# Moving the mixing matrices of a two-layer conditional residual kernel from GpSimd to VectorE

## The chip, the core and the metric

The kernel runs on one core of a Trainium2 chip. The metric is the device time of one launch in microseconds (us), here the median of three runs. The engines of the core work side by side and meet only at semaphores: TensorE (PE; its weight loads are PEld), VectorE (DVE), ScalarE (ACT), GpSimd (POOL) and SyncE (SP), which here only issues DMAs.

## What is computed

There are 64 samples of 128 channels by 2048 positions, in float32. Both layers add their result to their input:

```
# layer 0: grouped convolution, 4 groups of 32 channels, 9 taps, plus a context column
x = x + conv1d(x, weight, groups=4, padding=4) + (c @ c_weight.T)[:, :, None] + bias[None, :, None]
# layer 1: per sample a mix of K = 8 matrices of 128 x 128
h   = gelu(c @ W0 + b0);  h = gelu(h @ W1 + b1);  att = softmax(h @ W2 + b2)       # [64, 8]
agg_w = einsum('bk,koi->boi', att, weight[..., 0]);  agg_b = att @ bias_k
x = x + einsum('boi,bih->boh', agg_w, x) + agg_b[:, :, None]
```

So each sample needs its own matrix of 128 x 128: the sum of eight fixed matrices, each times one attention weight, plus the identity for the residual. This is the **mixing matrix**. The attention weights and the bias column of all samples stand in `table`, 9 columns per sample.

## The kernel before, in words

**Precision.** TensorE works on a rounded type, so each operand is split in two: a rounded value ("hi") and its rest ("lo" = value minus hi). A product is hi*hi + hi*lo + lo*hi. For x, `x_hi` and `x_lo`; for the first layer's output y, `y_hi` and `y_lo`; the mixing matrix is stored as `mix_parts[., 0]` (hi) and `[., 1]` (lo).

**Stages of one sample s.** SP loads x(s) into `x_in`. ACT turns it into four phases, `x_ph` (`split_phases`, L508). DVE rounds it, `x_hi` (`round_x`, L595), and takes the rest, `x_lo` (`rest_x`, L601). PE convolves (`conv_step`, L429): 36 steps for each of four output phases g, the four running side by side in four row groups and each two steps behind the one before. The last 12 of the 36 steps read `x_lo`. ACT rounds the result out of PSUM, `y_hi` (`round_y`, L521), and DVE takes its rest, `y_lo` (`rest_y`, L612), four instructions each. The PSUM bank of phase g is free for the convolution of s+1 when `y_lo(s, g)` is made. Two samples later PE multiplies y by the mixing matrix (`mix_step`, L460, 12 steps per phase), and ACT adds the bias column from `par` and writes `z_out` (`take_z`, L534), which SP stores.

**The order.** Each engine runs the same software pipeline: a `slot` per sample, slots 0 to 7 written out, 8 to 59 in a hardware loop, the rest written out. An engine works through its slots strictly in order, so an instruction that waits holds up all behind it. Per slot s the order is: PE convolves s, then mixes s-2; ACT takes z(s-3), splits x(s+2), rounds y(s); DVE rounds x(s+1), takes the rest of x(s+1), then the four rests of y(s); SP loads the mixing matrix of s-1, stores z(s-3), loads x(s+4), stores the matrix of s. `x_in`, `x_ph`, `x_hi`, `x_lo` have two buffers each, so ACT may split x(s+2) only when `x_lo(s)` is made (the wait `x_lo_made` in `split_phases`).

**The mixing matrix** is made by GpSimd alone (`mix_matrix`, L731 to L763), for every sample: a copy of the sample's 9 columns to `par` (L734), two products of 128x512 (L739), a tree of three sums (L744 twice, L747), the identity added twice (L751, L754), and the rest (L757). It goes through DRAM (`mix_dram`) to be replicated into four row groups (`mix_rep`, four DMAs, L290), and TensorE needs it two slots after the sample's convolution. A `par` buffer is reused after four samples (the wait on `z_read`).

**The start.** During the convolution of sample 0 the small network runs between its steps. DVE fills the attention columns of `table` (L664) and, after the four rests of y(0), finishes the bias column (`finish_table`, L676 to L680), upon which GpSimd copies it to `par[0]` (L763).

Of the kernel before, what the change touches and what calls it, by code (L numbers as in the profile page):

```python
# [5 lines left out]
F32 = mybir.dt.float32  # L6
# [48 lines left out]
def cond_resid_kernel(nc, x, cond, bias, conv_w, ctx_w, w0, b0, w1, b1, w2, b2, mix_w, mix_b, out):  # L55
# [15 lines left out]
    with ExitStack() as stack:  # L71
        def sb(name, shape, dt=F32):
            return stack.enter_context(nc.sbuf_tensor(name, shape, dt))

        def sem(name):
            return stack.enter_context(nc.semaphore(name))
# [125 lines left out]
        par_made = sem("par_made")  # L202
        par_first = sem("par_first")
        prod_made = sem("prod_made")
        mix_sum = sem("mix_sum")
        mix_hi_made = sem("mix_hi_made")
        mix_made = sem("mix_made")
# [42 lines left out]
        def _(sp):  # L250
            def ahead(*values):

                for v in values:
                    if not isinstance(v, int):
                        sp.compute_val(v)
                return values
# [11 lines left out]
            def store_mix(s):  # L268

                if not exists(s):  # L270
                    return
                b = buf(s)
                made, taken = ahead(done(s), DMA * G * uses(s))
                sp.wait_ge(mix_made, made)

                at_least(sp, mix_loaded[b], taken)
                sp.dma_start(mix_dram[b][:, :, :], mix_parts[b][:, :, :].bitcast(F32)).then_inc(mix_stored[b], DMA)
# [310 lines left out]
        def _(dve):  # L588
# [42 lines left out]
            def rest_half(h):  # L631
# [39 lines left out]
                                    ALU.add).then_inc(table_made, 1)  # L671
            rest_x((0, 1))

            def finish_table():
                dve.wait_ge(table_made, 2)
                nc.vector.tensor_tensor(aggb_prod, aggb_prod, table[:, :, 0:NK], ALU.mult).then_inc(table_made, 1)  # L676
                dve.wait_ge(table_made, 3)
                nc.vector.tensor_reduce(agg_b[:, :], aggb_prod, AX.X, ALU.add).then_inc(table_made, 1)
                dve.wait_ge(table_made, 4)
                nc.vector.tensor_tensor(table[:, :, NK:NK + 1].rearrange("p s a -> p (s a)"), agg_b[:, :],  # L680
                                        ctx_c[:, :], ALU.add).then_inc(table_made, 1)
# [26 lines left out]
        def _(pool):  # L708
# [15 lines left out]
            def mix_matrix(s):  # L724

                if not exists(s):
                    return

                at_least(pool, z_read, done(s, 2, lag=-U))
                if is_sample(s, 0):  # L730
# [16 lines left out]
                nc.gpsimd.tensor_tensor(mix_sum_f[:, :], mix_prod[:, 0, :], mix_prod[:, 1, :],  # L747
                                        ALU.add).then_inc(mix_sum, 1)
                pool.wait_ge(mix_sum, done(s, 3))

                nc.gpsimd.tensor_tensor(mix_f[:, :], mix_sum_f[:, :], ident[:, :], ALU.add)  # L751

                at_least(pool, mix_stored[buf(s)], DMA * uses(s))
# [3 lines left out]
                nc.gpsimd.tensor_tensor(mix_parts[buf(s)][:, 1, :], mix_f[:, :],  # L757
                                        mix_parts[buf(s)][:, 0, :].bitcast(F32),
                                        ALU.subtract).then_inc(mix_made, 1)
                pool.wait_ge(mix_made, done(s))  # L760
                if is_sample(s, 0):
                    pool.wait_ge(table_made, 5)
                    nc.gpsimd.tensor_copy(par[0][:, NK:PC], table[:, 0, NK:PC]).then_inc(par_made, 1)  # L763
# [27 lines left out]
```

## Time and profile before

| | |
|---|---|
| median of 3 runs | 729.33 us (728.32 to 730.14) |
| profiled execution, own time | 728.89 us |
| its span | 726.9 us |
| PE busy | 716.2 us, 99% |
| PEld busy | 701.7 us, 97% |
| DVE busy | 462.2 us, 64% |
| ACT busy | 601.3 us, 83% |
| POOL busy | 546.9 us, 75% |
| mean granted TensorE clock | 0.998 |

The span goes from the first to the last instruction; some 2 us of the execution lie around it. Busy time is the time in which an engine had an instruction running, waits inside an instruction included. TensorE's matmuls overlap, so a busy PE need not be at its peak; idle weight loads show a stall sooner.

### The profile page before, as it was taken

The numbers are of one execution on the slowest core, as the hardware profiler recorded it, in microseconds if no ns is written. First come the engines' busy times: TensorE is split into PE (matmuls) and PEld (weight loads), VectorE is DVE, ScalarE is ACT, GpSimd is POOL, SyncE is SP. The second block draws the span as 40 slices with busy tenths as digits, with TensorE's granted clock in tenths as the row PEclk, the third lists the DMA queues.
The fourth block names the chain that finished last, engine by engine and source line by source line (L and its number), as shares of the span: only waits on it lengthen the run. The fifth ranks groups of instructions, "written<-read, shape, count | busy, mean of one in ns | idle before, by whom it ended". The sixth has DMA issues, their size and how long they took to land.

```text
span 726.9 us, 29222 instructions
## 1 busy us (share of the span) xinstructions
PE 716.2 (99%) x12417; PEld 701.7 (97%) x12417; DVE 462.2 (64%) x411; ACT 601.3 (83%) x458; POOL 546.9 (75%) x592
## 2 busy tenths in 40 slices
PE   8999999999999999999999999999999999999996
PEld 6799999999999999999999999999999999999996
DVE  4897676576776675575575575575575575575543
ACT  5988888878888888888988888888888988888843
POOL 2799999999999999967767767767767767767750
PEclk9999999999999999999999999999999999999999
DMA  6345858768777877877787778777777767767546
GB/s 208 140 152 200 274 202 281 244 213 298 251 250 261 274 253 248 285 244 246 268 280 260 251 272 294 244 238 275 245 242 275 245 238 275 245 243 271 191 151 243
DMA packets 66551, 177.56 MB, mean 244 GB/s; under 512 B 7437, under 2 KB 50008, under 8 KB 50264
## 3 DMA queue, kind: packets, MB, share of 16 engines
q1 hardware_dynamic: 66002, 176.93, 71.5%
q8 instruction: 25, 0.41, 0.2%
q10 hardware_dynamic: 518, 0.17, 0.1%
q14 instruction: 6, 0.05, 0.0%
HBM read 101.57 MB, written 75.50 MB: 244 GB/s over the span
## 4 chain that ended last, share of the span: by engine, by line
PE 81%; POOL 11%; DMA 5%; SPq 1%; issue 1%; DVE 0%; ACT 0%; DVEq 0%; POOLq 0%; ACTq 0%
PE ps L429 60%; PE ps L460 21%; POOL mix_prod L744 4%; POOL mix_prod L739 4%; DMA mix_dram<-mix_parts 3%; POOL mix_sum_f L747 1%; DMA x_in<-in_x_dram 1%; SPq L290 1%; POOL mix_f L751 1%; DMA mix_rep<-mix_dram 1%; POOL mix_parts L757 1%; POOL mix_parts L754 0%; POOL par L734 0%; POOL par L763 0%; ACT x_hi L512 0%
## 5 line engine op out<-in xcount | busy, mean ns | idle before, releaser
L429 PE MATMUL ps<-x_hi,cw_hi 32*128 32x512 f32 x3072 | 406.0, 387 | 0.8 <-ACT x_hi L512 0.5
L429 PE MATMUL ps<-x_hi,cw_lo 32*128 32x512 f32 x3072 | 405.0, 386 | 0.0
L508 ACT ACTIVATE x_ph<-x_in 128x2560 f32<-128x2560 f32 x63 | 318.7, 5060 | 2.7 <-DMA x_in<-in_x_dram 2.2
L612 DVE TENSOR_TENSOR y_lo<-ps,y_hi 128x512 fp32r<-128x512 f32 x256 | 159.1, 683 | 241.1 <-ACT y_hi L521 241.1
L429 PE MATMUL ps<-x_lo,cw_hi 32*128 32x512 f32 x3072 | 275.6, 385 | 0.0
L429 PEld LDWEIGHTS ps<-x_lo,cw_hi 32*128 32x128 f32 x3072 | 240.0, 183 | 2.3 <-issue 0.8
L429 PEld LDWEIGHTS ps<-x_hi,cw_hi 32*128 32x128 f32 x3072 | 219.5, 184 | 3.8 <-issue 1.6
L429 PEld LDWEIGHTS ps<-x_hi,cw_lo 32*128 32x128 f32 x3072 | 219.1, 184 | 1.6 <-issue 0.2
L460 PE MATMUL ps<-y_hi,mix_rep 32*128 32x512 f32 x2048 | 215.1, 384 | 2.1 <-DMA mix_rep<-mix_dram 2.1
L534 ACT ACTIVATE z_out<-ps,par 128x1024 f32<-128x1024 f32 x124 | 146.5, 1242 | 74.5 <-PE ps L460 74.5
L601 DVE TENSOR_TENSOR x_lo<-x_ph,x_hi 128x2560 fp32r<-128x2560 f32 x63 | 190.0, 3016 | 2.1
L460 PEld LDWEIGHTS ps<-y_hi,mix_rep 32*128 32x128 f32 x2048 | 182.3, 183 | 4.3 <-issue 1.8
L744 POOL TENSOR_TENSOR mix_prod<-mix_prod 128x512 f32<-128x512 f32 (+1 forms) x128 | 165.3, 1291 | 10.0
L521 ACT ACTIVATE y_hi<-ps 128x512 fp32r<-128x512 f32 x256 | 132.9, 603 | 32.1 <-PE ps L429 32.0
L460 PE MATMUL ps<-y_lo,mix_rep 32*128 32x512 f32 x1024 | 158.1, 384 | 0.0
L739 POOL TENSOR_TENSOR mix_prod<-mixw_t,par 128x512 f32<-128x512 f32 x128 | 147.2, 1171 | 5.2
L734 POOL COPY par<-table 128x9 f32 (+1 forms) x63 | 68.9, 1094 | 108.0 <-ACT z_out L534 102.2
L460 PEld LDWEIGHTS ps<-y_lo,mix_rep 32*128 32x128 f32 x1024 | 125.2, 183 | 0.6
L595 DVE CAST x_hi<-x_ph 128x2560 fp32r<-128x2560 f32 x63 | 100.9, 1601 | 0.3 <-ACT x_ph L508 0.3
L747 POOL TENSOR_TENSOR mix_sum_f<-mix_prod 128x128 f32<-128x128 f32 x64 | 45.4, 710 | 5.0
L751 POOL TENSOR_TENSOR mix_f<-mix_sum_f,ident 128x128 f32<-128x128 f32 x64 | 40.8, 637 | 5.0
L754 POOL TENSOR_TENSOR mix_parts<-mix_sum_f,ident 128x128 fp32r<-128x128 f32 x64 | 39.9, 623 | 0.0
(79 smaller groups left out, 94.9 us busy)
## 6 DMA issues: line engine op xcount, KB each, us to landing
x_in<-in_x_dram SPq DMA_DIRECT2D x64, 1024.0 KB, 7.0
out_dram<-z_out SPq DMA_DIRECT2D x63, 1024.0 KB, 5.0
mix_rep<-mix_dram SPq DMA_DIRECT2D x256, 128.0 KB, 2.7
mix_dram<-mix_parts SPq DMA_DIRECT2D x64, 128.0 KB, 5.7
out_dram<-x_in SPq DMA_DIRECT2D x2, 512.0 KB, 4.0
z_out<-in_L_cond_weight_dram SPq DMA_DIRECT2D x1, 512.0 KB, 4.0
cw_nat<-in_L_cond_weight_dram SPq DMA_DIRECT2D x1, 144.0 KB, 2.2
w_sb<-in_L_cond_W_dram ACTq DMA_DIRECT2D x2, 64.0 KB, 5.0
```

The lines of the kernel that those rows point to most:

```text
L429: mm = pe.matmul(y_at(s)[:, g, :], w[rows, m, :], x_at(xx[buf(s)], rows, m), start=i == 0, stop=i == CONV - 1)
L460: mm = pe.matmul(z_at(s)[:, r, :], rep_at(s)[rows, g, h, :], yy[s[1]][rows, g, :], start=i == 0, stop=i == MIX - 1)
L508: nc.scalar.activation(x_ph[buf(s)][:, :, :, :], by_lane(x_in[buf(s)]), ACT.Copy).then_inc(x_split_ph, 1)
L521: nc.scalar.activation(y_hi[s[1]][:, g, :], y_at(s)[:, g, :], ACT.Copy).then_inc(y_hi_made, 1)
L534: nc.scalar.activation(out_lanes(z_out[buf(s)], pair), z_lanes(z_at(s), pair), ACT.Identity, bias=par[s[1]][:, NK:NK + 1]).then_inc(z_read, 1)
L595: nc.vector.tensor_copy(x_hi[buf(s)][:, :, :, :], x_ph[buf(s)][:, :, :, :]).then_inc(x_hi_made, 1)
L601: nc.vector.tensor_tensor(x_lo[buf(s)][:, :, :, :], x_ph[buf(s)][:, :, :, :], x_hi[buf(s)][:, :, :, :].bitcast(F32), ALU.subtract).then_in ...
L612: nc.vector.tensor_tensor(y_lo[s[1]][:, g, :], y_at(s)[:, g, :], y_hi[s[1]][:, g, :].bitcast(F32), ALU.subtract).then_inc(y_lo_made, 1)
L734: nc.gpsimd.tensor_copy(par[s[1]][:, :], table[:, number(s), :]).then_inc(par_made, 1)
L739: nc.gpsimd.tensor_tensor(mix_prod[:, ks, :], mixw_t[:, ks, :], par[s[1]][:, ks].unsqueeze(2).broadcast_to([P, NK // 2, P]), ALU.mult).the ...
L744: nc.gpsimd.tensor_tensor(mix_prod[:, 0:half, :], mix_prod[:, 0:half, :], mix_prod[:, half:2 * half, :], ALU.add).then_inc(mix_sum, 1)
L747: nc.gpsimd.tensor_tensor(mix_sum_f[:, :], mix_prod[:, 0, :], mix_prod[:, 1, :], ALU.add).then_inc(mix_sum, 1)
```

## The change

GpSimd makes the mixing matrices of samples 0 and 1 only (`FIRST = 2`), and between the two it finishes the bias column of `table`, by a tree of sums in place of DVE's reduction. DVE makes the matrices of samples 2 to 63, that of s+1 at the end of slot s, by another sequence of instructions: a copy of 9 columns, eight multiply-adds of 128x128 into two alternating accumulators, two sums, one rest. It begins the first of them only when GpSimd has copied `par[0]` and `par[1]` (`par_made` at 2). DVE's order within a slot changes too: the rests of y(s) now stand ahead of the rest of x(s+1), save in slot 1. SP waits for either maker's semaphore.

```diff
-                made, taken = ahead(done(s), DMA * G * uses(s))
-                sp.wait_ge(mix_made, made)
+                made, taken = ahead(done(s) if by_pool(s) else done(s, lag=-FIRST), DMA * G * uses(s))
+                if by_pool(s):
+                    sp.wait_ge(mix_first_made, made)
+                else:
+                    sp.wait_ge(mix_made, made)
...
-            rest_x((0, 1))
-
-            def finish_table():
-                dve.wait_ge(table_made, 2)
-                nc.vector.tensor_tensor(aggb_prod, aggb_prod, table[:, :, 0:NK], ALU.mult).then_inc(table_made, 1)
-                dve.wait_ge(table_made, 3)
-                nc.vector.tensor_reduce(agg_b[:, :], aggb_prod, AX.X, ALU.add).then_inc(table_made, 1)
...
+            def mix_matrix(s):
+
+                if not exists(s) or by_pool(s):
+                    return
+
+                at_least(dve, z_read, done(s, 2, lag=-U))
+                if is_sample(s, FIRST):
+                    dve.wait_ge(par_made, FIRST)
+                a = par[s[1]]
+                nc.vector.tensor_copy(a[:, :], table[:, number(s), :]).then_inc(par_made, 1)
+                dve.wait_ge(par_made, done(s))
+
+                for k in range(NK):
+                    part = (mix_even, mix_odd)[k % 2]
+                    if k == 0:
+                        nc.vector.tensor_scalar(part[:, :], mixw_t[:, k, :], a[:, k:k + 1], None,
+                                                ALU.mult).then_inc(mix_term, 1)
+                        continue
+                    if k >= 2:
+                        dve.wait_ge(mix_term, done(s, NK, lag=-FIRST - 1) + k - 1)
+                    nc.vector.scalar_tensor_tensor(part[:, :], mixw_t[:, k, :], a[:, k:k + 1],
+                                                   ident[:, :] if k == 1 else part[:, :],
+                                                   ALU.mult, ALU.add).then_inc(mix_term, 1)
+                dve.wait_ge(mix_term, done(s, NK, lag=-FIRST))
+                nc.vector.tensor_tensor(mix_f[:, :], mix_even[:, :], mix_odd[:, :], ALU.add).then_inc(mix_sum, 1)
+
+                at_least(dve, mix_stored[buf(s)], DMA * uses(s))
+                nc.vector.tensor_tensor(mix_parts[buf(s)][:, 0, :], mix_even[:, :], mix_odd[:, :],
+                                        ALU.add).then_inc(mix_sum, 1)
+                dve.wait_ge(mix_sum, done(s, 2, lag=-FIRST))
+                nc.vector.tensor_tensor(mix_parts[buf(s)][:, 1, :], mix_f[:, :],
+                                        mix_parts[buf(s)][:, 0, :].bitcast(F32),
+                                        ALU.subtract).then_inc(mix_made, 1)
+                dve.wait_ge(mix_made, done(s, lag=-FIRST))
 
             def slot(s):
-                if not is_sample(s, 0):
-                    round_x(after(s, 1))
+                if is_sample(s, 0):
+                    for g in range(G):
+                        rest_y(s, g)
+                    return
+                round_x(after(s, 1))
+                if is_sample(s, 1):
                     rest_x(after(s, 1))
                 for g in range(G):
                     rest_y(s, g)
-                if is_sample(s, 0):
-                    finish_table()
-
+                if not is_sample(s, 1):
+                    rest_x(after(s, 1))
+                mix_matrix(after(s, 1))
+
+            rest_x((0, 1))
             pipeline(dve, slot)
...
+            def finish_table():
+                pool.wait_ge(table_made, 2)
+                nc.gpsimd.tensor_tensor(aggb_prod, aggb_prod, table[:, :, 0:NK], ALU.mult).then_inc(agg_made, 1)
+                for n, half in enumerate((4, 2, 1)):
+                    pool.wait_ge(agg_made, n + 1)
+                    nc.gpsimd.tensor_tensor(aggb_prod[:, :, 0:half], aggb_prod[:, :, 0:half],
+                                            aggb_prod[:, :, half:2 * half], ALU.add).then_inc(agg_made, 1)
+                pool.wait_ge(agg_made, 4)
+                pool.wait_ge(ctx_made, 1)
+                nc.gpsimd.tensor_tensor(table[:, :, NK], aggb_prod[:, :, 0], ctx_c[:, :], ALU.add).then_inc(agg_made, 1)
+                pool.wait_ge(agg_made, 5)
+                nc.gpsimd.tensor_copy(par[0][:, NK:PC], table[:, 0, NK:PC]).then_inc(par_made, 1)
 
             pool.wait_ge(table_made, 1)
             pool.wait_ge(mixw_copied, 1)
-            pipeline(pool, mix_matrix)
+            mix_matrix((0, 0))
+            finish_table()
+            mix_matrix((0, 1))
```

## Rows read from the trace of the kernel before

**Rows 1.** The page, busy time, share of the span and instructions of each engine.
```profile
PE 716.2 (99%) x12417; PEld 701.7 (97%) x12417; DVE 462.2 (64%) x411; ACT 601.3 (83%) x458; POOL 546.9 (75%) x592
```

**Rows 2.** The page, the chain that ended last, share of the span by engine.
```profile
PE 81%; POOL 11%; DMA 5%; SPq 1%; issue 1%; DVE 0%; ACT 0%; DVEq 0%; POOLq 0%; ACTq 0%
```

**Rows 3.** The same chain in order of time, 280 to 304 us: start, us, what.
```profile
288.14 1.38 PE ps L460 x25
...
299.02 1.38 PE ps L460 x25
```

**Rows 4.** Timeline of PEld: start, us, instruction, count, [idle before <-releaser].
```profile
46.53 0.18 PEld L429 LDWEIGHTS ps<-x_hi,cw_hi 32*128 32x128 f32 x1 [0.67 <-issue]
...
99.93 0.18 PEld L460 LDWEIGHTS ps<-y_hi,mix_rep 32*128 32x128 f32 x1 [1.47 <-DMA mix_rep<-mix_dram]
...
144.84 0.18 PEld L460 LDWEIGHTS ps<-y_hi,mix_rep 32*128 32x128 f32 x1 [1.47 <-issue]
```

**Rows 5.** Timeline of POOL at the start.
```profile
31.37 0.47 POOL L747 TENSOR_TENSOR mix_sum_f<-mix_prod 128x128 f32<-128x128 f32 x1
...
33.20 0.49 POOL L757 TENSOR_TENSOR mix_parts<-mix_f,mix_parts 128x128 fp32r<-128x128 f32 x1
...
35.02 0.19 POOL L734 COPY par<-table 128x9 f32<-128x9 f32 x1
...
43.22 2.92 POOL L747 TENSOR_TENSOR mix_sum_f<-mix_prod 128x128 f32<-128x128 f32 x1
```

**Rows 6.** Timeline of DVE at the start.
```profile
31.62 0.76 DVE L676 TENSOR_TENSOR z_out<-z_out,table 128x512 f32<-128x512 f32 x1
...
35.07 2.83 DVE L601 TENSOR_TENSOR x_lo<-x_ph,x_hi 128x2560 fp32r<-128x2560 f32 x1
37.81 2.48 DVE L612 TENSOR_TENSOR y_lo<-ps,y_hi 128x512 fp32r<-128x512 f32 x4
...
42.57 3.25 DVE L601 TENSOR_TENSOR x_lo<-x_ph,x_hi 128x2560 fp32r<-128x2560 f32 x1
```

**Rows 7.** Timeline of POOL, one matrix with little beside it on DVE.
```profile
337.99 2.04 POOL L739 TENSOR_TENSOR mix_prod<-mixw_t,par 128x512 f32<-128x512 f32 x2
340.10 2.11 POOL L744 TENSOR_TENSOR mix_prod<-mix_prod 128x512 f32<-128x512 f32 x2
342.29 0.46 POOL L747 TENSOR_TENSOR mix_sum_f<-mix_prod 128x128 f32<-128x128 f32 x1
```

**Rows 8.** Timeline of DVE, two small copies in a row.
```profile
18.34 0.29 DVE L647 COPY ctxw_t<-ps 128x128 f32<-128x128 f32 x1 [0.36 <-PE ps L369]
18.55 0.16 DVE L648 COPY mixb_t<-ps 128x8 f32<-128x8 f32 x1
```

**Rows 9.** Timeline of ACT: one split that waited for DVE, one that none followed idle.
```profile
37.99 5.13 ACT L508 ACTIVATE x_ph<-x_in 128x2560 f32<-128x2560 f32 x1 [0.55 <-DVE x_lo L601]
...
151.30 5.06 ACT L508 ACTIVATE x_ph<-x_in 128x2560 f32<-128x2560 f32 x1 [0.43 <-DMA x_in<-in_x_dram]
156.25 2.05 ACT L521 ACTIVATE y_hi<-ps 128x512 fp32r<-128x512 f32 x4
```

**Rows 10.** Timeline of DVE, the steady state.
```profile
156.97 2.48 DVE L612 TENSOR_TENSOR y_lo<-ps,y_hi 128x512 fp32r<-128x512 f32 x4 [4.58 <-ACT y_hi L521]
...
341.99 2.48 DVE L612 TENSOR_TENSOR y_lo<-ps,y_hi 128x512 fp32r<-128x512 f32 x4 [4.14 <-ACT y_hi L521]
344.39 1.48 DVE L595 CAST x_hi<-x_ph 128x2560 fp32r<-128x2560 f32 x1
345.90 2.83 DVE L601 TENSOR_TENSOR x_lo<-x_ph,x_hi 128x2560 fp32r<-128x2560 f32 x1
```

**Rows 11.** Timeline of PEld: all four phases of a convolution have begun.
```profile
344.85 0.23 PEld L429 LDWEIGHTS ps<-x_hi,cw_hi 32*128 32x128 f32 x4
```

**Rows 12.** Windows at the end: stretch, us, busy of each engine, PEclk, DMA.
```profile
719.00:721.00 2.00, 1.62 (x20) 1.06 (x12) 0.66 (x2) 1.21 (x2) 0.00 (x0) 1.00 0.94 385
...
723.00:725.00 2.00, 0.00 (x0) 0.00 (x0) 0.00 (x0) 0.00 (x0) 0.00 (x0) 0.79 1.00 406
```

More of the change, by code:

```diff
@@ L19 @@
 MIX_LATE = 2
+FIRST = 2
 OUTER, INNER = (0, 8, 1, 9, 2, 10, 3, 11), (4, 5, 6, 7)
@@ L116, in cond_resid_kernel @@
         mix_sum_f = sb("mix_sum_f", [P, P])
+        mix_f_first = sb("mix_f_first", [P, P])
+        mix_even = sb("mix_even", [P, P])
+        mix_odd = sb("mix_odd", [P, P])
         mix_f = sb("mix_f", [P, P])
@@ L203, in cond_resid_kernel @@
         par_first = sem("par_first")
+        agg_made = sem("agg_made")
         prod_made = sem("prod_made")
+        tree_sum = sem("tree_sum")
+        mix_hi_made = sem("mix_hi_made")
+        mix_first_made = sem("mix_first_made")
+        mix_term = sem("mix_term")
         mix_sum = sem("mix_sum")
-        mix_hi_made = sem("mix_hi_made")
         mix_made = sem("mix_made")
@@ L221, in is_sample, with by_pool @@
             return isinstance(s[0], int) and number(s) == b
+        def by_pool(s):
+            return isinstance(s[0], int) and number(s) < FIRST
         def pipeline(eng, slot):
@@ L671, in _ @@
                                     ALU.add).then_inc(table_made, 1)
-            rest_x((0, 1))
-            def finish_table():
-                dve.wait_ge(table_made, 2)
-                nc.vector.tensor_tensor(aggb_prod, aggb_prod, table[:, :, 0:NK], ALU.mult).then_inc(table_made, 1)
-                dve.wait_ge(table_made, 3)
-                nc.vector.tensor_reduce(agg_b[:, :], aggb_prod, AX.X, ALU.add).then_inc(table_made, 1)
-                dve.wait_ge(table_made, 4)
-                nc.vector.tensor_tensor(table[:, :, NK:NK + 1].rearrange("p s a -> p (s a)"), agg_b[:, :],
-                                        ctx_c[:, :], ALU.add).then_inc(table_made, 1)
@@ L724, in mix_matrix @@
             def mix_matrix(s):
-                if not exists(s):
-                    return
-                at_least(pool, z_read, done(s, 2, lag=-U))
                 if is_sample(s, 0):
@@ L744, in mix_matrix @@
                     nc.gpsimd.tensor_tensor(mix_prod[:, 0:half, :], mix_prod[:, 0:half, :],
-                                            mix_prod[:, half:2 * half, :], ALU.add).then_inc(mix_sum, 1)
-                    pool.wait_ge(mix_sum, done(s, 3, lag=-1) + n + 1)
+                                            mix_prod[:, half:2 * half, :], ALU.add).then_inc(tree_sum, 1)
+                    pool.wait_ge(tree_sum, done(s, 3, lag=-1) + n + 1)
                 nc.gpsimd.tensor_tensor(mix_sum_f[:, :], mix_prod[:, 0, :], mix_prod[:, 1, :],
[L748 to L753, printed above, removed]
+                                        ALU.add).then_inc(tree_sum, 1)
+                pool.wait_ge(tree_sum, done(s, 3))
+                nc.gpsimd.tensor_tensor(mix_f_first[:, :], mix_sum_f[:, :], ident[:, :], ALU.add)
                 nc.gpsimd.tensor_tensor(mix_parts[buf(s)][:, 0, :], mix_sum_f[:, :], ident[:, :],
@@ L756, in mix_matrix @@
                 pool.wait_ge(mix_hi_made, done(s))
-                nc.gpsimd.tensor_tensor(mix_parts[buf(s)][:, 1, :], mix_f[:, :],
+                nc.gpsimd.tensor_tensor(mix_parts[buf(s)][:, 1, :], mix_f_first[:, :],
                                         mix_parts[buf(s)][:, 0, :].bitcast(F32),
[L759 to L763, printed above, removed]
+                                        ALU.subtract).then_inc(mix_first_made, 1)
+                pool.wait_ge(mix_first_made, done(s))
+            def finish_table():
[10 more added lines that the diff above has]
+                nc.gpsimd.tensor_copy(par[0][:, NK:PC], table[:, 0, NK:PC]).then_inc(par_made, 1)
             pool.wait_ge(table_made, 1)
             pool.wait_ge(mixw_copied, 1)
-            pipeline(pool, mix_matrix)
+            mix_matrix((0, 0))
+            finish_table()
+            mix_matrix((0, 1))
 _INS = ["x", "cond_128", "fside_S_0", "L0_cond_weight", "L0_cond_c_weight", "L1_cond_W0", "L1_cond_b0",
```

## The prediction

> **What bounds the kernel now.** The page's busy times come first: PE has work 99% of the span and PEld 97% [rows 1]. Whatever the change does to GpSimd's or VectorE's busy time is worth nothing by itself; it counts only where it takes away or adds an idle moment of TensorE. The shares of the chain seem to say otherwise, POOL 11% and DMA 5% [rows 2]: the chain ran along GpSimd while matrix followed matrix. But PE worked beside it, so 16% is no gain that is to be had. The chain in order of time gives the pace behind it: a sample from 288.14 to 299.02, 10.88 us [rows 3], and 64 x 10.88 = 696.3 of the 726.9 us. The rest is start, end and stalls. The stalls stand in PEld's timeline: 1.47 us each at 99.93 and 144.84, where a mixing matrix came late (the first names its DMA), and 0.67 us at 46.53, where the convolution of sample 3 begins [rows 4]. So the most that earlier matrices can bring behind the start is some 2.9 us, 0.4%.
>
> **What goes.** GpSimd needed from 35.0 to past 46.1 for matrix 1, the sum of L747 included [rows 5], as long as TensorE needs for a sample: it never got ahead. After the change the matrix of s+1 is made in DVE's slot s, and SP can store and replicate it more than a slot before TensorE wants it. Both late matrices go: **-2.9 us**.
>
> **GpSimd's matrices 0 and 1, and the wait between.** Which VectorE instructions hold up GpSimd? L747 takes 0.46 us alone [rows 7], but 2.92 us when it starts during an `x_lo` of 42.57 to 45.82 [rows 5, 6]; that `x_lo` itself takes 3.25 against 2.83 us [rows 6, 10]. So an instruction of either waits until that of the other is through, and they take turns. Now the start. Before, VectorE finished the table from 31.62 on, which left GpSimd room to end matrix 0 at 33.20 + 0.49 = 33.7 [rows 5, 6]. After, VectorE goes from its `y_lo(0)` to `x_hi(2)` at 31.6. It waits for L747 (to 31.8) and lasts 1.48 us, to 33.3; L751 then gets its turn (0.46, to 33.8); `x_lo(2)` takes 2.83 us, to 36.6; L754 and L757 end at 37.6. Matrix 0 is 3.9 us later, about when TensorE wants it (a small term, hidden below). Then `finish_table` on GpSimd: sums of 512 and 256 columns for 2.11 us (as L744), one of 128 for 0.46, two of 64 and under for at most 0.46 each, say 0.3, a copy of 0.19, six gaps of 0.08: 3.8 us, to 41.4; the copy of `par[1]`, 0.19, to 41.6 [rows 5, 7]. VectorE is through with `y_lo(1)` at about 38.9 and waits for that copy, 2.7 us. Behind it in VectorE's queue stand `x_hi(3)` and `y_lo(2)`, and for these TensorE waits.
>
> **VectorE's matrix, by itself.** No row has a multiply-add of 128 columns. A copy of 128 columns takes 0.29 us, the next instruction follows after 0.21, one of 8 columns takes 0.16 [rows 8]. Eight terms 0.21 apart and the last one whole: 7 x 0.21 + 0.29 = 1.8; the copy and its wait 0.3; the first sum 0.2, the second whole 0.3, the rest 0.3, waits 0.1: **3.0 us**. Bounds: 2.5 us if all but the ends follow at 0.16; 4.9 if none of the 12 overlaps (12 x 0.41, with waits of 0.12). I take 3.0, by the row that has the width.
>
> **VectorE's matrix 2 beside GpSimd's matrix 1.** GpSimd begins matrix 1 at the same 41.6: 2.04 + 2.11 + 4 x 0.46 = 6.0 us of its own [rows 7], eight instructions. If the two take turns, VectorE waits for each of these eight: 3.0 + 6.0 = 9.0 us, to 50.6. If VectorE keeps its turn over instructions that follow with no gap, it waits for the first one alone: 4 us, to 45.6; below that, 3.0 with no wait at all. The rows of an `x_lo` behind an `x_hi` show turns taken, and I take 9.0. Then `x_hi(3)`, 1.48, to 52.1, and the first `y_lo(2)`, 0.68, to 52.8. There the convolution of sample 3 starts; before it was 46.53 [rows 4]: **+6.3 us** (bounds: -1.0, where TensorE's own 45.5 decides, to +6.5). The stall of 0.67 and the lateness of matrix 0 lie inside it.
>
> The Trainium skill (SBUF — State Buffer, Who interferes with whom) has a rule for this: VectorE and GpSimd share one port pair as an exclusive lock for a whole instruction, and besides an instruction with two SBUF inputs a copy or `tensor_scalar` can take it. The trace shows it for casts and for `tensor_tensor`; by the rule all 12 instructions of the new sequence would take part, which is the 9.0 and not the 4.
>
> **The order within a slot.** The rests of y now stand ahead of the rest of x, and ACT's split of x(s+2) waits for `x_lo(s)`. That closes a ring over ACT and DVE, once around per sample: split to `y_hi`, 156.25 - 151.30 = 4.95 us (the split's 5.06 us less an overlap of 0.11); `y_hi` to `y_lo`, 156.97 - 156.25 = 0.72; four `y_lo` to the next instruction, 344.39 - 341.99 = 2.40; `x_lo` 2.83; from its end to the split, 37.99 - 37.90 = 0.09, and that case had a second wait beside it; the hand-over can hardly be under 0.02 [rows 6, 9, 10]. The sum is 10.92 to 10.99, against TensorE's 10.88 [rows 3]. Before, `x_lo` lay ahead of `y_lo` and was no part of such a ring. So ACT and DVE, neither of them full, together set a pace up to 0.1 us slower than TensorE's. `y_hi` to `y_lo` is 0.03 shorter in one slot of four of the loop, I leave that aside and take the low end, 0.04. The slack is small: the fourth `y_lo` ends at 344.47 and the convolution that needs it begins at 344.85, 0.38 us [rows 10, 11], and the late start uses it up. 60 samples x 0.04 = **+2.4 us** (bounds: 0, if a split is 0.04 faster with GpSimd quiet, to 6).
>
> **VectorE's own load** is 2.40 + 2.83 + 3.0 + 1.48 + 0.1 = 9.8 us per sample, under 10.88, so a matrix of up to 4.1 us is hidden. SP's order is kept; its wait for a matrix is over early.
>
> **Sum**, against the profiled execution's 728.9: -2.9 + 6.3 + 2.4 = +5.8, so 734.7. The median of runs lies 0.4 above the profiled one, so 735.1; I say **735.0 us**.
>
> **The clock.** The granted clock is 1.00 while TensorE works, up to its last matmul before 721, and 0.79 in 723 to 725 [rows 12], a fall to the lower level (1.2 of 2.4 GHz) within the stretch, after TensorE had been idle. At that level a sample lasts twice as long, so half a sample at it costs some 2 to 3 us. TensorE would be idle for 6 to 7 us before 52.8, longer than from 721 to the end of that stretch. It isn't in the sum, but it is the upper part of the range. The Trainium skill (TensorE: Matmul & The Clock Gate, Why this matters for your kernels) warns of idle gaps between bursts of matmuls for the same reason.
>
> **Rivals.** *A, my forecast* (late start, ring slower than TensorE): 732.5 to 740. Chance 0.42. *B, VectorE keeps its turn*: it is through with matrix 2 at 45.6, the convolution starts at 47.8, +1.3; with the ring +2.4 and -2.9, 729.3 + 0.8 = 730.1. For it: the terms follow one another without a gap, which no row of two such instructions shows; against it the turns in [rows 5, 6]. 0.26. *C, the other side, faster*: the ring closes in 10.88 or less, by a split quicker than the rows of [rows 9], and the start costs at most 1 us. The late matrices are then the one thing that changes, with half a microsecond from `y_lo(2)` made ahead of `x_lo(3)`: 729.3 - 2.9 + 0.5 = 727, down to 725.5. It decides at a ring of 10.88. 0.16. *D, ring free but start late*: 729.3 + 6.3 - 2.9 = 732.7. 0.10. *E, VectorE the bound*: the 12 instructions serial, 4.9 us, make a slot of 11.7; 0.8 x 60 = 48, so 775. It decides from 4.1 us on. 0.06.
>
> **Numbers.** A change under 0.3%, 2.2 us, can't be told from none: faster is under 727.1, slower over 731.5. Faster: most of C and a little of B, 0.15. Slower: A, E, most of D and the upper edge of B, 0.57. Same: 0.28. The range goes from C's middle to A's upper end with the clock: 726.5 to 740; A's own is 732.5 to 740.
>
> **What would show it.** Right: GpSimd's matrix 0 ends near 37.6 instead of 33.7; a VectorE wait of 2 to 3 us for `par[1]`'s copy; a PEld idle stretch of 5 to 7 us before 53; multiply-adds stretched to 0.5 us and more there and 0.2 apart later; no idle PEld before L460 behind it; `x_lo` followed by a split within 0.1 us, no idle ACT before `y_hi`, and a sample of 10.90 to 10.99. Wrong: a sample of 10.88 with ACT idle before `y_hi` (the ring is no bound), or `x_hi(3)` rounded before 47 (no queue at the start), or a sample over 11 (VectorE the bound).

## The result and the profile after

| | before | after |
|---|---|---|
| median of 6 runs, us | 728.83 (727.90 to 730.48) | 732.98 (732.05 to 734.38) |
| ratio after to before, 95% interval | | 1.0058 (1.0037 to 1.0078) |
| profiled execution, us | 728.9 | 732.69 |
| its span, us | 726.9 | 730.9 |

The kernel became slower by 0.58%, and the interval excludes both no change and 0.3%. The page of the changed kernel, busy times and shares of the chain; the rows of before are [rows 1] and [rows 2]:

```profile
PE 718.3 (98%) x12417; PEld 703.7 (96%) x12417; DVE 632.3 (87%) x1152; ACT 602.5 (82%) x458; POOL 27.9 (4%) x39
...
PE 94%; POOL 2%; DVE 1%; DMA 1%; issue 0%; ACT 0%; DVEq 0%; SPq 0%; POOLq 0%; ACTq 0%
```

GpSimd went from 547 to 28 us and VectorE from 462 to 632 us. POOL and DMA left the chain, 16% down to 3%. None of this says where 4 us went: PE was and is the chain. The waits do (engine, line, waited for: us in total, times, longest us), first those of the kernel before, then those of the changed one:

```profile
ACT y_hi L521 <- PE ps L429: 32.0, 61, 5.4
...
ACT x_ph L508 <- DVE x_lo L601: 0.5, 1, 0.5
```

```profile
DVE y_lo L627 <- ACT y_hi L536: 58.5, 61, 2.6
ACT x_ph L523 <- DVE x_lo L616: 57.7, 59, 1.2
...
ACT y_hi L536 <- PE ps L444: 14.2, 5, 5.4
```

ACT's split now waits for `x_lo` 59 times, where it did so once. And ACT waits for TensorE before `y_hi` 5 times, where it did so 61 times. That is the ring of the prediction: a closed chain of waits, in which each engine is held up by the other once per sample. In the steady state it looks like this, ACT first, VectorE behind it (start, us, instruction, [idle before <-releaser]):

```profile
306.09 5.10 ACT L523 ACTIVATE x_ph<-x_in 128x2560 f32<-128x2560 f32 x1 [1.08 <-DVE x_lo L616]
311.10 2.03 ACT L536 ACTIVATE y_hi<-ps 128x512 fp32r<-128x512 f32 x4
...
317.10 5.11 ACT L523 ACTIVATE x_ph<-x_in 128x2560 f32<-128x2560 f32 x1 [1.17 <-DVE x_lo L616]
```

```profile
311.79 2.49 DVE L627 TENSOR_TENSOR y_lo<-ps,y_hi 128x512 fp32r<-128x512 f32 x4 [1.10 <-ACT y_hi L536]
314.19 2.81 DVE L616 TENSOR_TENSOR x_lo<-x_ph,x_hi 128x2560 fp32r<-128x2560 f32 x1
...
317.33 0.34 DVE L708 SCALAR_TENSOR_TENSOR mix_odd<-mixw_t,par,ident 128x128 f32<-128x128 f32 x1
317.59 0.34 DVE L708 SCALAR_TENSOR_TENSOR mix_even<-mixw_t,par,mix_even 128x128 f32<-128x128 f32 x1
```

Once around: split to `y_hi` 5.01, `y_hi` to `y_lo` 0.69, `y_lo` to `x_lo` 2.40, `x_lo` 2.81, to the next split 0.10, in all 11.01 us for this sample; the mean of 48 samples is 10.947. Both engines show idle time, 1.1 us on each, and still each always waits for the other.

TensorE's share of it is too small for the views of waits, which leave out idle time of 0.15 us and less. The busy time of its weight loads shows it (stretch, us, busy of PE, PEld, DVE, ACT, POOL, then PEclk, DMA share, GB/s), before and after:

```profile
480.00:600.00 120.00, 120.00 (x2124) 119.69 (x2120) 73.79 (x66) 103.28 (x78) 83.61 (x100) 1.00 0.73 253
```

```profile
480.00:600.00 120.00, 120.00 (x2112) 118.97 (x2108) 106.38 (x199) 102.80 (x78) 0.00 (x0) 1.00 0.73 251
```

The weight loads are idle 1.03 us instead of 0.31 in these eleven samples. That is 0.066 us more per sample, the whole difference between 10.947 and 10.88.

The start: TensorE's weight loads, to be held against the stall of 0.67 us in [rows 4]:

```profile
43.68 0.18 PEld L475 LDWEIGHTS ps<-y_hi,mix_rep 32*128 32x128 f32 x1 [2.07 <-DMA mix_rep<-mix_dram]
...
49.23 0.18 PEld L444 LDWEIGHTS ps<-x_hi,cw_hi 32*128 32x128 f32 x1 [2.94 <-DVE x_hi L610]
```

These two are the last that the view of waits lists for the weight loads until 720.8. The two late matrices of [rows 4], at 99.93 and 144.84, are gone. The same stretch on VectorE, with its matrix 2 drawn out:

```profile
39.67 0.17 DVE L697 COPY par<-table 128x9 f32<-128x9 f32 x1 [2.34 <-POOL par L776]
39.88 0.96 DVE L703 TENSOR_SCALAR mix_even<-mixw_t,par 128x128 f32<-128x128 f32 x1
40.77 1.14 DVE L708 SCALAR_TENSOR_TENSOR mix_odd<-mixw_t,par,ident 128x128 f32<-128x128 f32 x1
41.83 1.42 DVE L708 SCALAR_TENSOR_TENSOR mix_even<-mixw_t,par,mix_even 128x128 f32<-128x128 f32 x1
...
45.52 0.61 DVE L708 SCALAR_TENSOR_TENSOR mix_odd<-mixw_t,par,mix_odd 128x128 f32<-128x128 f32 x1
...
46.70 0.29 DVE L718 TENSOR_TENSOR mix_parts<-mix_f,mix_parts 128x128 fp32r<-128x128 f32 x1
47.02 1.49 DVE L610 CAST x_hi<-x_ph 128x2560 fp32r<-128x2560 f32 x1
48.43 2.48 DVE L627 TENSOR_TENSOR y_lo<-ps,y_hi 128x512 fp32r<-128x512 f32 x4
```

And on GpSimd, beside it:

```profile
32.22 3.04 POOL L794 TENSOR_TENSOR mix_parts<-mix_sum_f,ident 128x128 fp32r<-128x128 f32 x1
35.34 0.46 POOL L797 TENSOR_TENSOR mix_parts<-mix_f_first,mix_parts 128x128 fp32r<-128x128 f32 x1
...
39.72 2.04 POOL L781 TENSOR_TENSOR mix_prod<-mixw_t,par 128x512 f32<-128x512 f32 x2
41.84 2.06 POOL L786 TENSOR_TENSOR mix_prod<-mix_prod 128x512 f32<-128x512 f32 x2
43.98 0.46 POOL L789 TENSOR_TENSOR mix_sum_f<-mix_prod 128x128 f32<-128x128 f32 x1
```

Windows of the changed kernel (stretch, us, busy of PE, PEld, DVE, ACT, POOL, then PEclk, DMA share, GB/s):

```profile
9.00:12.40 3.40, 3.40 (x30) 2.92 (x31) 2.74 (x2) 3.19 (x3) 0.00 (x0) 0.50 1.07 393
48.00:50.00 2.00, 0.74 (x12) 0.75 (x16) 2.00 (x4) 0.00 (x0) 0.00 (x0) 1.00 0.57 167
50.00:53.40 3.40, 3.40 (x36) 3.40 (x35) 3.40 (x3) 2.39 (x2) 0.00 (x0) 0.50 1.02 280
53.40:56.00 2.60, 2.60 (x49) 2.60 (x48) 2.53 (x11) 2.27 (x1) 0.00 (x0) 1.00 0.43 170
```

After the waits the granted clock is 0.50, TensorE's lower level of 1.2 GHz, from 50.0 to 53.4, although PE is busy throughout.

**Where the 4.0 us between the spans went.** T(s) is the moment at which the first `y_hi` of sample s begins.

| stretch | before, us | after, us | difference |
|---|---|---|---|
| up to T(0) | 27.95 | 26.84 | -1.1 |
| T(0) to T(3) | 27.23 | 32.47 | +5.2 |
| T(3) to T(63) | 655.93 | 655.90 | 0.0 |
| T(63) to the end | 15.8 | 15.7 | -0.1 |

The first row is in all likelihood chance: the clock rises during the first convolution at 12.4 in one run and at about 14.2 in the other (last section), and two kernels with the changed start, e4 and e9 below, had T(0) at 28.0 and 28.2. The interval of the medians, 2.7 to 5.7 us, holds both 4.1 and 5.2, so it doesn't decide it. The third row is two effects of equal size. Before, 60 x 10.88 = 652.8, and 3.1 of late matrices. After, 59 at a mean of 10.946, and one of 10.06 at the end, where no x is left to split and `y_hi`, no longer held back by the ring, begins earlier behind TensorE: 3.1 above 652.8 as well.

### The profile page after: what moved, and what is told of

Its sections match the earlier page's. It is cut to its first block, busy times and chain, and to the rows that moved or that the text cites. A ratio compares the mean times of both kernels' runs of the same rounds, so it can differ in the third digit from the quotient of the medians.

```text
span 730.9 us, 29507 instructions
## 1 busy us (share of the span) xinstructions
PE 718.3 (98%) x12417; PEld 703.7 (96%) x12417; DVE 632.3 (87%) x1152; ACT 602.5 (82%) x458; POOL 27.9 (4%) x39
## 4 chain that ended last, share of the span: by engine, by line
PE 94%; POOL 2%; DVE 1%; DMA 1%; issue 0%; ACT 0%; DVEq 0%; SPq 0%; POOLq 0%; ACTq 0%
PE ps L444 70%; PE ps L475 24%; DMA x_in<-in_x_dram 1%; POOL mix_prod L786 1%; POOL mix_prod L781 0%; POOL mix_parts L794 0%; DVE mix_odd L708 0%; DVE mix_even L708 0%; POOL mix_f_first L793 0%; POOL z_out L807 0%; DVE x_hi L610 0%; ACT x_hi L527 0%; POOL z_out L804 0%; PE ps L399 0%; DVE mix_even L703 0%
## 5 line engine op out<-in xcount | busy, mean ns | idle before, releaser
L444 PE MATMUL ps<-x_hi,cw_hi 32*128 32x512 f32 x3072 | 437.0, 389 | 3.3 <-DVE y_lo L627 2.5
L444 PE MATMUL ps<-x_hi,cw_lo 32*128 32x512 f32 x3072 | 436.1, 388 | 0.0
L444 PEld LDWEIGHTS ps<-x_hi,cw_hi 32*128 32x128 f32 x3072 | 327.0, 184 | 9.4 <-DVE x_hi L610 2.9
L444 PEld LDWEIGHTS ps<-x_hi,cw_lo 32*128 32x128 f32 x3072 | 313.5, 184 | 0.9 <-issue 0.2
L536 ACT ACTIVATE y_hi<-ps 128x512 fp32r<-128x512 f32 x256 | 131.8, 606 | 14.2 <-PE ps L444 14.2
L610 DVE CAST x_hi<-x_ph 128x2560 fp32r<-128x2560 f32 x63 | 95.1, 1509 | 12.4 <-DVE mix_parts L718 10.8
L708 DVE SCALAR_TENSOR_TENSOR mix_even<-mixw_t,par,mix_even 128x128 f32<-128x128 f32 x186 | 66.0, 355 | 0.0
L708 DVE SCALAR_TENSOR_TENSOR mix_odd<-mixw_t,par,mix_odd 128x128 f32<-128x128 f32 x186 | 65.5, 352 | 0.0
L708 DVE SCALAR_TENSOR_TENSOR mix_odd<-mixw_t,par,ident 128x128 f32<-128x128 f32 x62 | 22.3, 359 | 0.0
L703 DVE TENSOR_SCALAR mix_even<-mixw_t,par 128x128 f32<-128x128 f32 x62 | 18.5, 298 | 2.2
L718 DVE TENSOR_TENSOR mix_parts<-mix_f,mix_parts 128x128 fp32r<-128x128 f32 x62 | 18.1, 292 | 2.2
L712 DVE TENSOR_TENSOR mix_f<-mix_even,mix_odd 128x128 f32<-128x128 f32 x62 | 18.1, 292 | 2.1
```

Source lines behind the costliest of these rows:

```text
L444: mm = pe.matmul(y_at(s)[:, g, :], w[rows, m, :], x_at(xx[buf(s)], rows, m), start=i == 0, stop=i == CONV - 1)
L536: nc.scalar.activation(y_hi[s[1]][:, g, :], y_at(s)[:, g, :], ACT.Copy).then_inc(y_hi_made, 1)
L610: nc.vector.tensor_copy(x_hi[buf(s)][:, :, :, :], x_ph[buf(s)][:, :, :, :]).then_inc(x_hi_made, 1)
L703: nc.vector.tensor_scalar(part[:, :], mixw_t[:, k, :], a[:, k:k + 1], None, ALU.mult).then_inc(mix_term, 1)
L708: nc.vector.scalar_tensor_tensor(part[:, :], mixw_t[:, k, :], a[:, k:k + 1], ident[:, :] if k == 1 else part[:, :], ALU.mult, ALU.add).the ...
L712: nc.vector.tensor_tensor(mix_f[:, :], mix_even[:, :], mix_odd[:, :], ALU.add).then_inc(mix_sum, 1)
```

## The experiments

My theory: the whole loss is the start (VectorE's matrix 2 stretched by GpSimd's matrix 1, and what hangs on it), and behind it the ring costs what the late matrices gave. The rivals: that the ring is not due to the order but to VectorE's load or to the matrices; and that the start's loss lies in the order or the table.

**e1_order_back.** The old order in the slots, all else as after.

```diff
                 round_x(after(s, 1))
-                if is_sample(s, 1):
-                    rest_x(after(s, 1))
+                rest_x(after(s, 1))
                 for g in range(G):
                     rest_y(s, g)
-                if not is_sample(s, 1):
-                    rest_x(after(s, 1))
```

> The changed kernel with one thing undone: in every slot VectorE takes the rest of x(s+1) ahead of the rests of y(s), as before the change; it still makes the matrices from sample 2 on. Theory (a ring over ACT and VectorE, split - y_hi - y_lo - x_lo - split, sets 10.95 us a sample): the ring is open, ACT no longer waits for x_lo (57.7 us idle before L523 fall to under 5), a sample lasts 10.88, and the time falls by 3 to 4 us against the changed kernel, to about 729.5. Rival (VectorE's own load, 87% busy, or its many small instructions slow the pace): nothing falls, a sample stays at 10.93 to 10.95, 733.

Measured: 733.15 us (6 runs), ratio 1.0062 (1.0038 to 1.0087) to before. ACT in the steady state, and TensorE's wait at the start:

```profile
307.90 5.16 ACT L523 ACTIVATE x_ph<-x_in 128x2560 f32<-128x2560 f32 x1
313.29 2.07 ACT L536 ACTIVATE y_hi<-ps 128x512 fp32r<-128x512 f32 x4 [0.23 <-PE ps L444]
```

```profile
52.14 0.28 PEld L444 LDWEIGHTS ps<-x_hi,cw_hi 32*128 32x128 f32 x1 [6.36 <-issue]
```

The mechanism held: a sample takes 10.880 us, T(3) to T(63) is 652.80 = 60 x 10.880 with not one stall, the split starts unheld and `y_hi` waits for TensorE. TensorE's weight loads are busy for 119.69 of the 120 us from 480 to 600 again, as before the change. The time missed by 3.6 us, all of it at the start: T(0) to T(3) is 36.08 instead of 32.47. In slot 2, VectorE is late already, and `x_lo(3)`, 2.8 us, now stands ahead of the `y_lo(2)` for which TensorE waits. The granted clock falls to 0.50 at 50.4, while TensorE still stands, and stays there for 6.8 us. The new order costs 3.1 us in the loop and saves 3.6 in one slot. Part of the 3.6 is the shorter spell of low clock, 3.4 us instead of 6.8.

**e2_pad_in_ring** and **e3_pad_off_ring.** One more VectorE instruction per sample, inside the ring or outside it, one profiled run each and so without an interval.

```diff
+        pad = sb("pad", [P, 512])
...
                 if not is_sample(s, 1):
+                    if exists(after(s, 1)):
+                        nc.vector.memset(pad[:, :], 0.0)
                     rest_x(after(s, 1))
```

> The changed kernel with one VectorE memset of 128x512 more per slot, just ahead of the rest of x, that is inside the ring. Ring theory: its 0.49 us adds to each of about 60 samples, a sample lasts 11.43 us and the whole 762 us (+29), though VectorE is idle for 1.1 us in each slot. Rival (the pace is VectorE's load or TensorE's): it fits in the idle time, at most +3.

```diff
                 mix_matrix(after(s, 1))
+                if not is_sample(s, 1) and exists(after(s, 1)):
+                    nc.vector.memset(pad[:, :], 0.0)
```

> The same memset, 0.49 us, at the end of VectorE's slot behind the mixing matrix, outside the ring. Ring theory: VectorE's idle time of 1.1 us in front of y_lo shrinks by it and a sample stays at 10.95; the whole is within 2 us of the changed kernel, 733. Rival (VectorE's load sets the pace): the same +29 as with the memset inside the ring.

Measured: 760.68 us with the memset in the ring, 732.67 with it off the ring. VectorE in e2, and ACT's wait over the whole of it:

```profile
311.06 2.48 DVE L628 TENSOR_TENSOR y_lo<-ps,y_hi 128x512 fp32r<-128x512 f32 x4 [1.12 <-ACT y_hi L537]
313.60 0.48 DVE L736 MEMSET pad<- 128x512 f32 x1
314.01 2.76 DVE L617 TENSOR_TENSOR x_lo<-x_ph,x_hi 128x2560 fp32r<-128x2560 f32 x1
```

```profile
ACT x_ph L524 <- DVE x_lo L617: 102.9, 59, 1.8
```

A sample takes 11.432 us in e2, 0.485 more than after: the memset's own 0.48 (11.432 - 10.947). In e3 it takes 10.949. VectorE idles 1.1 us just before its `y_lo` in e2, so this isn't a lack of VectorE's time; where the same instruction stands decides between 28 us and nothing. That shows the ring, and that VectorE's load is hidden, against rival E.

**e4_table_back.** VectorE finishes the table again, as before; the rest as after.

```diff
                     for g in range(G):
                         rest_y(s, g)
+                    finish_table()
                     return
...
             def finish_table():
-                pool.wait_ge(table_made, 2)
...
+                pool.wait_ge(table_made, 5)
                 nc.gpsimd.tensor_copy(par[0][:, NK:PC], table[:, 0, NK:PC]).then_inc(par_made, 1)
```

> The changed kernel with the table's bias column finished by VectorE again, behind y_lo(0), as before the change. Theory (queue at the start: VectorE stands behind GpSimd's matrix 0, its finish of the table and the copy of par[1], 2.3 us idle): VectorE works 1.7 us itself, GpSimd's matrix 0 ends 2 to 3 us earlier, the idle PEld stretch of 2.07 us ahead of mix 0 goes, that ahead of the convolution of sample 3 falls from 2.94 to about 2, and the time falls by 2 to 3 us to about 730.5. Rival (turns with GpSimd's matrix 1 are the whole cost of the start): matrix 2 on VectorE still ends after 46 and the time stays within 1 us of 733.

Measured: 730.47 us (10 runs), ratio 1.0028 (1.0012 to 1.0044), as expected. The one stall left in the start, and GpSimd's first half of matrix 1:

```profile
47.83 0.18 PEld L444 LDWEIGHTS ps<-x_hi,cw_hi 32*128 32x128 f32 x1 [2.09 <-DVE x_hi L610]
```

```profile
35.14 4.51 POOL L791 TENSOR_TENSOR mix_prod<-mixw_t,par 128x512 f32<-128x512 f32 x2
```

GpSimd begins matrix 1 at 35.1 instead of 39.7. Matrix 0 isn't late (its stall of 2.07 is gone), T(0) to T(3) is 29.37, and the granted clock stays at 1.00 behind the stall of 2.09. So of the start's +5.2 us, 3.1 belong to the table on GpSimd, the spell of low clock included. The other 2.1 are about what the turns still cost: matrix 2 takes 5.5 us here (40.06 to 45.59).

**e5_pool_later.** GpSimd begins matrix 1 when VectorE is through with matrix 2 (one profiled run).

```diff
-                    nc.gpsimd.tensor_copy(par[s[1]][:, :], table[:, number(s), :]).then_inc(par_made, 1)
...
             finish_table()
+            nc.gpsimd.tensor_copy(par[1][:, :], table[:, 1, :]).then_inc(par_made, 1)
+            pool.wait_ge(mix_made, 1)
             mix_matrix((0, 1))
```

> The changed kernel, but GpSimd begins its matrix 1 only when VectorE has made matrix 2 (the copy of par[1] stays where it is). VectorE's first matrix then runs with GpSimd quiet. Theory (turns with GpSimd stretch it from 3.3 to 7.3 us): it takes 3.3 us, y_lo(2) starts 4 us earlier (44.4 instead of 48.4), the idle PEld stretch ahead of the convolution of sample 3 goes; matrix 1 is late in its place, with a stall of 2 to 5 us ahead of mix 1. Rival (the stretch is a first-time cost of these instructions, of code or of the table): VectorE's first matrix still takes 7 us.

Measured: 734.53 us. VectorE, which began at the same time as in the changed kernel, and TensorE:

```profile
39.56 0.17 DVE L697 COPY par<-table 128x9 f32<-128x9 f32 x1 [2.32 <-POOL par L818]
...
42.45 0.29 DVE L718 TENSOR_TENSOR mix_parts<-mix_f,mix_parts 128x128 fp32r<-128x128 f32 x1
...
44.19 2.48 DVE L627 TENSOR_TENSOR y_lo<-ps,y_hi 128x512 fp32r<-128x512 f32 x4
```

```profile
58.85 0.28 PEld L475 LDWEIGHTS ps<-y_hi,mix_rep 32*128 32x128 f32 x1 [5.08 <-DMA mix_rep<-mix_dram]
```

Alone the matrix takes 3.2 us (39.56 to 42.74), beside GpSimd 7.3 (39.67 to 46.99). The wait for `x_hi(3)` is gone, and T(0) to T(3) is 28.41, against 32.47 in the changed kernel and 27.23 before. But matrix 1 is late instead: TensorE stands for 5.08 us, and the granted clock is 0.50 from 56.8 to 63.6. The two matrices compete for the same microseconds, and either order costs.

**e6_order_only.** The kernel before with nothing but the new order (one profiled run).

```diff
                     round_x(after(s, 1))
+                if is_sample(s, 1):
                     rest_x(after(s, 1))
                 for g in range(G):
                     rest_y(s, g)
+                if not is_sample(s, 0) and not is_sample(s, 1):
+                    rest_x(after(s, 1))
```

> The kernel before with the new order within a slot alone: GpSimd makes all matrices, VectorE takes the rests of y(s) ahead of the rest of x(s+1) from slot 2 on. Ring theory: the ring is there without any matrix on VectorE, and GpSimd stretches x_lo inside it (mean 3.02 against 2.82), so a sample lasts 10.95 or more, 11.1 in the mean; the stall of 0.67 at sample 3 goes and the two late matrices may go too as TensorE is slower; 735 to 745. Rival (the order costs only together with VectorE's matrices): within 2 us of before, 728.

Measured: 733.86 us, 1.1 under the range that was expected.

```profile
ACT x_ph L508 <- DVE x_lo L601: 70.3, 60, 2.4
```

```profile
306.02 5.09 ACT L508 ACTIVATE x_ph<-x_in 128x2560 f32<-128x2560 f32 x1 [1.07 <-DVE x_lo L601]
...
317.02 5.08 ACT L508 ACTIVATE x_ph<-x_in 128x2560 f32<-128x2560 f32 x1 [1.21 <-DVE x_lo L601]
```

The ring stands there with GpSimd making all matrices, at a mean of 10.95 a sample from sample 12 to 60, where a mean of 11.1 was expected. So VectorE's matrices have no part in it: that rival falls. T(3) to T(63) is 659.15, 3.2 more than in the changed kernel, and most of that lies between 122 and 168 us, where four samples take 11.2 to 11.95 and `x_lo`, now in the ring, takes 3.1 to 3.9 us beside GpSimd.

**e7_best_f2** and **e8_best_f4.** The pieces that the runs so far favour: the table as in e4, and y ahead of x only in the slots in which VectorE is late: slot 2 for e7; slots 2 and 4 for e8, where GpSimd makes four matrices (and waits for a buffer's last store before it fills it again).

```diff
-                if is_sample(s, 1):
+                y_first = any(is_sample(s, b) for b in (2,))
+                if not y_first:
                     rest_x(after(s, 1))
                 for g in range(G):
                     rest_y(s, g)
-                if not is_sample(s, 1):
+                if y_first:
                     rest_x(after(s, 1))
```

> The changed kernel with the table finished by VectorE and the rests of y ahead of the rest of x in slot 2 alone, where VectorE is late; from slot 3 on the old order. If ring and start are the two costs and independent: the start of the kernel with the table back (stall 2.09), then 10.88 a sample and no late matrix: 730.5 - 3.1 = 727.4, or 0.999 of before. If they are not independent (a late start that only the new order mends): 729 to 731.

> The same, but GpSimd makes matrices 0 to 3 and VectorE takes over at sample 4, with the rests of y first in slots 2 and 4. Theory of turns: VectorE's first matrix meets GpSimd's matrix 3 and is stretched the same way; it costs a stall of 1 to 2 us ahead of the convolution of sample 5 instead of sample 3; the start is that of before or better; 726.5 to 728. Rival (the start is costly because several things are late there at once): no stall at the hand-over, 725.5.

Measured: e7 727.76 us (12 runs), ratio 1.0000 (0.9982 to 1.0018); e8 727.85, 0.9992 (0.9973 to 1.0011). Both loops run at 10.88 to 10.89. In e7 (first fence) the gain of the late matrices is spent on two stalls, the second where the order switches back. In e8 (second fence) it goes to matrices that SP brought late:

```profile
46.80 0.18 PEld L444 LDWEIGHTS ps<-x_hi,cw_hi 32*128 32x128 f32 x1 [2.12 <-DVE x_hi L610]
...
59.41 0.18 PEld L444 LDWEIGHTS ps<-x_hi,cw_hi 32*128 32x128 f32 x1 [1.49 <-issue]
```

```profile
86.11 0.82 SPq L292 DMA_DIRECT2D mix_dram<-mix_parts  x1
96.04 1.74 SPq L305 DMA_DIRECT2D mix_rep<-mix_dram  x4
...
101.03 0.18 PEld L475 LDWEIGHTS ps<-y_hi,mix_rep 32*128 32x128 f32 x1 [2.51 <-DMA mix_rep<-mix_dram]
```

VectorE had made this matrix, that of sample 5, by 74.1. SP issued its store at 86.1, behind a store of z and a load of x, and it took 9.9 us to land. That those big transfers are the cause no run shows alone. The stall that e8 was expected to show, ahead of the convolution of sample 5, did not come: VectorE's first matrix is drawn out there, too, but TensorE didn't wait for it. Instead the matrices of samples 3 and 5 were late, by 1.47 and 2.51 us. The profiled execution of e8 was the slowest of its twelve, 730.11 us, so it shows more loss than the median has.

**e9_early_store_f2** and **e10_early_store_f3.** So SP stores VectorE's matrices ahead of the transfers of its slot, with y ahead of x in slots 2 to 5; GpSimd makes two matrices in e9, three in e10.

```diff
                 load_mix(after(s, -1))
+                if not by_pool(s):
+                    store_mix(s)
                 store(after(s, -3))
                 load(after(s, AHEAD))
-                store_mix(s)
+                if by_pool(s):
+                    store_mix(s)
```

> A try at a version that beats both: the changed kernel with the table finished by VectorE, the rests of y first in slots 2 to 5 alone (so that the lateness of the start is not paid twice, as by the 1.49 us stall at 59.41 of the version with slot 2 alone), and SP storing VectorE's matrices ahead of its store of z and its load of x. Expected from the pieces: 727.8 less 0.8 for the second stall, plus 0.2 for the ring in three slots, 727.2; under the 0.3% that can be told from the kernel before (727.6). If the stores of the matrices were near to being late, it gains up to another 1 us.

> The same with GpSimd making matrices 0 to 2 and VectorE taking over at sample 3. If the stretch by turns costs as much one sample later, 727 to 728; if VectorE has more room there (it isn't late at slot 2 any more), the stall falls from 2.1 to under 1 and the time to 726.

Measured: e9 728.52 us (12 runs), ratio 0.9997 (0.9982 to 1.0011); e10 727.84 (12 runs), 0.9985 (0.9971 to 0.9998). The weight loads of e10:

```profile
57.15 0.18 PEld L447 LDWEIGHTS ps<-x_hi,cw_hi 32*128 32x128 f32 x1 [1.45 <-DVE x_hi L613]
...
91.61 0.18 PEld L447 LDWEIGHTS ps<-x_hi,cw_hi 32*128 32x128 f32 x1 [1.51 <-issue]
```

No matrix is late in e10; these two stalls of the start and of the switch are left. The first fell from 2.1 to 1.45 us, not to under 1. e9 missed its 727.2 by 1.3 us, and the second stall, which it was to save, was only put off: it is 1.49 us at 93.47, again where the order switches back, as in e7 at 59.41. e10 is 0.15% ahead of before, under the 0.3% that I called tellable. So the pieces of the change that are worth having bring the kernel to where it was, not past it.

## Why the prediction was right

Forecast 735.0 in a range of 726.5 to 740, with slower at 0.57 and rival A, the late start with the ring, at 0.42; measured 732.98, inside A's own 732.5 to 740. The number alone doesn't pick A: rival D, a late start without the ring, had 732.7, which is nearer than my 735.0. The waits and the experiments pick it. The mechanisms came as told; the sizes of the start and of the ring, and the clock left out of the sum, didn't.

**What bounds it, and what goes.** Late matrices: forecast -2.9, measured -3.1 (655.93 - 652.8). Right; e1 shows the loop without them and without the ring, 652.80.

**The start.** Forecast +6.3, measured +5.2, made of other parts. The convolution of sample 3 began at 49.23, not 52.8; measured from T(0), it is 3.8 us later than before (22.39 against 18.58). The steps were too dear by 2.5 us. I had GpSimd's matrix 0 end at 37.6. It ended at 35.8: 1.1 of the 1.8 is the earlier T(0), and most of the other 0.7 is that `x_lo(2)` followed `x_hi(2)` at once and was only 0.14 longer than alone (2.97 us), where I had it wait for a GpSimd instruction of 0.46. The table took 3.6 us (forecast 3.8), so matrix 2 began at 39.7 and not 41.6. And **matrix 2 took 7.3 us, not 9.0**. Of the eight small VectorE instructions each was drawn out, by 0.2 to 1.1 us, as many as GpSimd has instructions in its matrix; that is the turns as forecast. What failed is the addition: 3.0 + 6.0 takes it that nothing of the two lies beside each other, but the stretch was 4.1 us for 6.3 us of GpSimd (39.72 to 45.99). Which part of a waiting instruction is done meanwhile no run shows. e5 shows the cause: the same matrix at the same place takes 3.2 with GpSimd held back. Rival B, 4 us, was wrong. The lower bound was misread: the weight loads of [rows 4] would have gone on at 46.53 - 0.67 = 45.9 and not 45.5, so -0.7 and not -1.0. And one sign of being wrong was met all but by a hair: `x_hi(3)` was rounded from 47.02, against "before 47", since the queue at the start was shorter than forecast.

The Trainium skill (SBUF — State Buffer, Who interferes with whom) has the two engines lock each other out for a whole instruction. The trace agrees that all of VectorE's multiply-adds are drawn out. It doesn't bear out a price of the sum of both.

**Matrix 0.** I called its lateness a small term inside the later wait. It was a stall of 2.07 us of its own at 43.68, and together with the next, 2.94 at 49.23, it makes the 5.0 idle of the forecast 5 to 7. In time it cost little, since the convolution of sample 3 waited for VectorE anyhow. e5 has a similar stall (1.46), and e4, where the table is back, has none.

**The clock.** Left out of the sum, named as the upper part of the range. It came: 0.50 from 50.0 to 53.4, after two pauses of TensorE. From 49.23 to T(3) the changed kernel needs 10.08 us against 8.65 (46.53 to 55.18): +1.4, against an estimate of up to 1.7 for 3.4 us at half the clock. So the start is 3.8 of waiting and 1.4 of clock, where I forecast 6.3 of waiting and, beyond the sum, some of clock. That +5.2 came near +6.3 is luck in part: two errors that partly cancel.

**The ring.** Forecast 10.92 to 10.99, taken at 10.92, +2.4; measured 10.947, which is +4.0 over 59 samples, less the 0.8 given back in the one where the ring ends, +3.1. Right in kind, and e1, e2 with e3, and e6 show it three ways. The low end was the wrong one to take: the split to `y_hi` is 5.00 to 5.01 us and not 4.95, and the hand-over from `x_lo` to the split 0.10 in the sample shown.

**VectorE's matrix and load.** Forecast 3.0, measured 3.2: a multiply-add takes 0.34 and the next follows after 0.265, where the copies of [rows 8] gave 0.29 and 0.21. It is hidden, as e3 shows with half a microsecond more. Rival E was wrong.

**Rivals C and D** took the ring away, and the waits of ACT exclude that, whatever their times.

**The sum** by what was measured: -3.1 + 5.2 + 3.1 = +5.2, and -1.1 before T(0) makes 4.1, against 4.0 between the spans. In the medians the difference is 4.15. A profile that draws the clock's rise alike on both sides would by these terms show some 5.

## What to carry to other kernels

Ask of every reordering which wait it closes into a ring. Two engines, at 82% and 87%, set the pace here because each waited for the other once per sample; the proof was one extra instruction, placed in the ring (+28 us) and out of it (0).

When work moves between GpSimd and VectorE, count the stretch in which both run and who stands behind it; a matrix of 3.2 us took 7.3 there. The 3 us that no late matrix saves in the whole loop are less than the 5.2 that the late start costs.

An order is worth what the engine's lateness makes it: y ahead of x gains 3.6 us in the one slot where VectorE is late and loses 0.07 in each where it isn't. Switching between the orders isn't free either: a stall of 1.5 us stood at the switch in e7, e9 and e10.

## What I had not expected of the hardware

**The turns are uneven.** The introduction has the engines meet only at semaphores. VectorE and GpSimd also meet without one: the same twelve instructions take 3.2 us with GpSimd idle (e5) and 7.3 beside its matrix 1. GpSimd's instructions beside small VectorE ones kept their times: the two products 2.04, the sums 2.06 and 0.46, against 2.04, 2.11 and 0.46 in [rows 7]. VectorE's were drawn out to 0.54 to 1.42. Behind long VectorE instructions it is GpSimd that is drawn out: 3.04 instead of 0.46 (L794 at 32.22), and 4.51 instead of 2.04 in e4. In these rows the engine with the shorter instructions loses most. The long ones don't go free: `x_hi` takes 2.33 us at 40.21 in the kernel before, against 1.48 alone. How the turns are given beyond that stays open.

**Which pauses of TensorE the clock answered.** Pauses of 2.09 us (e4), 2.12 (e7) and 2.11 (e9) left the granted clock at 1.00. It was 0.50 for 3.4 us from 50.0 in the changed kernel, after pauses of 2.07 and 2.94 with 2.6 us of weight loads between them. It fell while TensorE still stood, and was 0.50 for 6.8 us, in e1 (pause of 6.36) and e5 (5.08). In e8 it was 0.53 over the stretch from 102.0 to 105.6, after a pause of 2.51.

**The rise of the clock in the first convolution** comes at another moment from run to run. In the changed kernel the granted clock is 0.50 from 9.0 to 12.4, then 1.00. The profile of the kernel before shows no 0.50 there, because its record of the clock begins only at 14.2; but its matmuls of the convolution take 0.62 us up to 13.5 and 0.39 at 14.5, and in the changed kernel that change comes at 12.4. T(0) differs by 1.1 us, as much as some of the terms that were argued about. e4 and e7 have the same instructions up to slot 3, and still T(0) is 27.96 in one and 26.96 in the other, with matmuls at 0.62 us up to 13.9 and up to 12.6. Both profiled kernels with the old start, before and e6, were among the late ones, so a small share of the change in it isn't excluded.
